# A Trainium2 kernel of two attentions and two ternary feed-forwards: the first attention written out in steps and joined to the feed-forward behind it, with its small sums moved between engines

## The chip, the cores and the metric

The kernel runs on one core of a Trainium2 chip. The metric is the device time of one execution in microseconds (us); the time before is the median of three runs. Engines are named as usual: TensorE (PE, with its weight loads as PEld), VectorE (DVE), ScalarE (ACT), GpSimd (POOL), and SyncE (SP), which issues every DMA here.

## What is computed

`x` and `ctx` are (16, 128, 256) in float32. Four residual blocks follow each other; the first two and the last are those that the change touches.

```python
def first_attention(q, k, v):            # 8 heads over the 256 "times", 16 rows of the 128 per head
    qn, kn = l2norm(q over the 16 rows), l2norm(k over the 16 rows)
    return softmax(5.0 * qn^T kn) applied to v

def ffn(x, w1, w2):                      # rms norm, rounding to 127 levels per row, ternary weights
    h = gelu(gelu(bitlinear(x, w1)))
    return bitlinear(h, w2)

x = x + first_attention(layernorm(x), ctx, ctx)
x = x + ffn(layernorm(x), L0_w1, L0_w2)                        # 256 -> 1024 -> 256
x = x + second_attention(layernorm(x), ctx, Wq, Wk, Wv, Wo)    # 16 heads, 4 of keys and values
x = x + gated_ffn(layernorm(x), w1, w2, w3)                    # 256 -> 2 x 704 -> 256
```

## The kernel before, in words

Line numbers are those of the kernel before, as in its profile.

The program has five parts. `prepare` loads, rounds and transposes the weights. `part_a` is the first attention. Then three parts run in one stream of steps: `part_ffn` "b" (the first feed-forward) from step 0, `part_c` (the second attention) from step 16, `part_ffn` "d" (the last feed-forward) from step 82. Each part is five programs, one per engine. Behind `prepare` and behind `part_a` stands a barrier (`end_part`): every engine drains and waits until all five have come.

**First attention.** The unit of work is a pair of heads of one batch, 4 units per batch, 64 in all. Each engine runs `body` over the units with fixed lags (SCORE = 21, VALUES = 22, COMBINE = 26, ...), counted by semaphores; of the four groups of 16 units, two are written out and two are a loop in hardware (`units`). Per batch:

- SyncE loads x (L292) and ctx (L294), copies the halves of ctx^T to `ctx_t` (L312), stores the split unit rows to a scratch in DRAM (L326), gathers them into stacks of three parts by 16 rows (L303, L306), loads x once more for the residual (L318) and copies the result to `x_rows` (L330), where the feed-forward reads it. 13 issues.
- VectorE: statistics of x (L460, L462, L464), centred and scaled rows (L430), a floor under the length sums (L449), the low half of ctx^T (L437), four copies of values into the stationaries `v_t` (L444, L445), unit rows (L470), their low half (L454), and the combine: four masked products out of the value bank (L412 to L419), a shuffle that brings the sums under the values (L422), and a reciprocal (L425).
- ScalarE: exponentials of 128 x 1024 scores (L361, four per batch), Ln and Exp for the deviation (L370, L372), squares (L378), Ln and Exp of the lengths (L385, L387), the high halves of ctx^T (L394) and of the unit rows (L400).
- TensorE: scores (L487, four matmuls per unit), transposes of ctx into one bank (L498), the length sum over a head's rows (L504, 32-bit, 512 columns), values (L518). A value matmul is 32-bit, has 32 stationary columns and 256 moving ones: 16 columns of values and 16 columns of ones, so that values and softmax sums come out of one matmul. Its output is one of four groups of 32 rows; heads 2r and 2r+1 share the group r and lie in the two halves of the bank. The two heads of a unit lie in two groups:

```python
for k in range(2):
    for j, h in enumerate(heads_of(v)):
        r, half = 32 * (h // 2), D * (h % 2)
        mm = eng.matmul(value_bank(vp)[r:r + 32, half:half + D], v_t[:, vb.lane % 4, k, h, :],
                        probs[:, q, j, k, :], start=(k == 0), stop=(k == 1))
```

- GpSimd: product of the two combined tiles (L346) and the residual add (L349).

**Feed-forwards.** Each step s handles several tiles of 128 rows (one batch each) at different depths: statistics of tile s, rounding of tile s - 2, the wide matmul of tile s - 4, and so on. VectorE runs a chain of one- and two-element instructions per step: in "b" L849 (floor under the variance), in "d" L852 and L855 (the variance times one number plus another), then L866, L876, L885, L891, L903 (the factors of the rounding), and L895 and L896 (a copy of the variance, and minus the mean). Their columns are two: one for a tile at its first rounding, one for a tile five steps older at its second (`pair`). GpSimd takes the power -1/2 (L766) and does the two roundings (L773, L780). ScalarE centres the rows in "d" (L791), VectorE in "b" (L910). In "d", L926 is gate times up (704 columns), L836 the largest absolute value of a row, L872 the residual.

## Time and profile before

| | us |
|---|---|
| median of 3 runs | 829.38 |
| lowest, highest | 828.62, 842.33 |
| profiled execution | 828.9 |
| its span | 827.2 |
| VectorE busy in it | 718.6 (87%) |
| TensorE busy | 681.0 (82%) |
| ScalarE busy | 650.9 (79%) |
| GpSimd busy | 475.1 (57%) |

The span runs from the first to the last instruction; the execution's own time is 1.7 us longer. The shares of busy time are means over stages with different limits, so each stage has to be read by itself. In a row of the timeline, `x8` merges eight instructions of one line, and the number in brackets is the time that the engine was idle ahead of it, with what released it.

### The profile page before, as it was taken

What the parts mean: (1) busy time and instruction counts of PE and PEld (TensorE: products, weight loads), DVE (VectorE), ACT (ScalarE), POOL (GpSimd) and SP (SyncE); (2) the same over time, 40 slices, a digit from 0 to 9 for tenths busy, and PEclk for the clock granted to TensorE, in tenths of its full rate; (3) what the DMA queues carried; (4) which work ended last, traced back from release to release, by engine and by line L of the source; (5) the groups of instructions that cost most, each with busy time, mean ns of one, the idle gap of its engine ahead of it and who ended that gap; (6) DMA issues with size and microseconds to landing.
All of it is one profiled execution on the core that took longest, in us unless ns stands there. A gap on an engine that the chain in (4) does not pass through costs nothing. (4 is left out here: it accounts for less than half of the span.)

```text
span 827.2 us, 16833 instructions
## 1 busy us (share of the span) xinstructions
PE 681.0 (82%) x4627; PEld 412.0 (50%) x4627; DVE 718.6 (87%) x1826; ACT 650.9 (79%) x2170; POOL 475.1 (57%) x639
## 2 busy tenths in 40 slices
PE   0175888888747767999999999999999999977876
PEld 0152333333313335566666666666666666644543
DVE  7667588998569968999999999999999999989996
ACT  0656687877439958999999999999999999977552
POOL 1410022122236778887788788878887888742453
PEclk9997699999969989999999999999999999999997
DMA  8501535544203436779877988788878877864235
GB/s 274 186 1 57 158 115 162 155 150 128 90 23 83 93 78 128 126 132 159 138 140 122 158 142 133 131 152 141 141 129 148 142 141 132 148 117 77 65 98 133
DMA packets 321999, 103.91 MB, mean 126 GB/s; under 512 B 286932, under 2 KB 321142, under 8 KB 321654
## 3 DMA queue, kind: packets, MB, share of 16 engines
q1 hardware_dynamic: 321910, 102.89, 60.4%
q8 instruction: 35, 0.57, 0.3%
q14 instruction: 54, 0.44, 0.2%
HBM read 22.10 MB, written 6.29 MB: 34 GB/s over the span
## 5 line engine op out<-in xcount | busy, mean ns | idle before, releaser
L1328 ACT ACTIVATE psum<-psum,arena 128x256 f32<-128x256 f32 x256 | 136.2, 533 | 18.7 <-DVE arena L1448 18.6
L1404 DVE SCALAR_TENSOR_TENSOR arena<-psum,arena 128x256 f16<-128x256 f32 x256 | 111.0, 475 | 1.1 <-ACT arena L1345 1.1
L1345 ACT ACTIVATE arena<-psum,arena 128x256 f16<-128x256 f32 x256 | 100.6, 476 | 8.4 <-issue 4.2
L1499 PE MATMUL psum<-wq_t,arena 128*128 128x512 f16 x384 | 94.6, 383 | 7.7 <-DMA arena<-arena 4.4
L1537 PE MATMUL psum<-arena 128*128 128x512 f16 x384 | 93.2, 378 | 8.9 <-DVE arena L1431 8.8
L1282 POOL TENSOR_TENSOR arena<-arena 128x512 f32<-128x512 f32 x64 | 81.1, 1267 | 28.0 <-DVE arena L1423 28.0
L1524 PE MATMUL psum<-arena 128*128 128x256 f16 x768 | 94.3, 273 | 1.7 <-DMA arena<-arena 1.0
L1552 PE MATMUL psum<-wo_t,arena 128*128 128x256 f16 x768 | 94.3, 273 | 0.1
L1552 PEld LDWEIGHTS psum<-wo_t,arena 128*128 128x128 f16 x768 | 75.0, 98 | 22.6 <-issue 0.6
L1313 POOL TENSOR_TENSOR arena<-arena 128x512 f16<-128x512 f32 x64 | 74.0, 1157 | 20.0 <-DVE arena L1448 19.9
L1524 PEld LDWEIGHTS psum<-arena 128*128 128x128 f16 x768 | 74.7, 98 | 11.6 <-DMA arena<-arena 2.6
L1423 DVE TENSOR_TENSOR arena<-psum,arena 128x1024 f32<-128x1024 f32 x64 | 78.3, 1224 | 2.4 <-PE psum L1499 2.4
L346 POOL TENSOR_TENSOR arena<-arena 128x256 f32<-128x256 f32 x16 | 11.9, 746 | 115.7 <-DVE arena L425 115.7
L1444 DVE TENSOR_REDUCE arena<-psum 128x4 f32<-128x1024 f32 x64 | 77.9, 1217 | 0.5 <-PE psum L1524 0.4
L361 ACT ACTIVATE arena<-psum 128x1024 f32<-128x1024 f32 x64 | 65.1, 1020 | 16.6 <-PE psum L487 16.6
L1359 ACT ACTIVATE arena<-psum 128x128 f32<-128x128 f32 x256 | 68.5, 305 | 11.8 <-DVE arena L1423 11.8
L518 PE MATMUL psum<-arena 128*32 128x256 f32 x512 | 69.0, 391 | 1.9 <-ACT arena L361 1.7
L1459 DVE SCALAR_TENSOR_TENSOR arena<-psum,arena 128x256 f32<-128x256 f32 x128 | 56.1, 480 | 10.8 <-ACT arena L1394 7.7
L1510 PE MATMUL psum<-wkv_t,ctx_t 128*128 128x256 f16 x384 | 53.7, 276 | 13.3 <-DVE arena L1463 12.4
L1359 ACT ACTIVATION_READ_ACCUMULATOR arena<-psum 128x1 f32 x256 | 61.1, 239 | 0.0
L1316 POOL TENSOR_TENSOR arena<-arena 128x256 f32<-128x256 f32 x64 | 46.4, 724 | 23.4 <-DVE arena L1459 23.4
L1499 PEld LDWEIGHTS psum<-wq_t,arena 128*128 128x128 f16 x384 | 37.4, 98 | 41.3 <-DMA arena<-arena 4.7
(191 smaller groups left out, 1661.2 us busy)
## 6 DMA issues: line engine op xcount, KB each, us to landing
arena<-split_scratch SPq DMA_DIRECT2D x96, 64.0 KB, 2.7
arena<-arena SPq DMA_TRANSPOSE x272, 3.3
arena<-in_x SPq DMA_DIRECT2D x32, 128.0 KB, 2.3
split_scratch<-arena SPq DMA_DIRECT2D x32, 128.0 KB, 1.8
arena<-in_L_ffn_w SPq DMA_DIRECT2D x2, 1024.0 KB, 7.0
x_rows<-in_L_xattn_Wq SPq DMA_DIRECT2D x1, 2048.0 KB, 14.3
ctx_t<-in_L_xattn_Wo SPq DMA_DIRECT2D x1, 2048.0 KB, 12.4
arena<-in_ctx SPq DMA_DIRECT2D x16, 128.0 KB, 2.2
```

The lines of the kernel that those rows point to most:

```text
L1282: eng.tensor_tensor(straight(q_rot[:, :, :]), straight(q_cs[:, 0, :, :]), swapped(q_cs[:, 1, :, :]), ALU.add).then_inc(S["q_rot"], 1)
L1313: eng.tensor_tensor(q_hl(u, 1), flat(q_rot[:, :, :]), q_hl(u, 0), ALU.subtract).then_inc(S["q_lo"], 1)
L1328: last = eng.activation(s_banks(u)[:, h, :], s_banks(u)[:, h, :], ACT.Exp, bias=bias[:, u % 2, h:h + 1], scale=r_q(u)[:, h:h + 1], accum_o ...
L1345: hi = eng.activation(p_hl[:, u % 2, 0, h, :], s_banks(u)[:, h, :], ACT.Copy, scale=share[:, u % 2, h:h + 1])
L1359: last = eng.activation(junk[:, h, :], Q_BANK[:, P * h:P * h + P], ACT.Square, accum_out=sums[:, u % 2, h:h + 1])
L1404: last = eng.scalar_tensor_tensor(p_hl[:, u % 2, 1, h, :], s_banks(u)[:, h, :], share[:, u % 2, h:h + 1], p_hl[:, u % 2, 0, h, :], ALU.mul ...
L1423: eng.tensor_tensor(q_cs[:, :, :, :], Q_BANK.rearrange("p (h d) -> p h d", h=SHARE).unsqueeze(1).broadcast_to([P, 2, SHARE, HEAD_DIM]), tu ...
L1444: eng.tensor_reduce(top[:, u % 2, :], s_banks(u), AX.X, ALU.max).then_inc(S["top"], 1)
L1499: mm = eng.matmul(Q_BANK, y_t[:, b % 2, x, k, :], c.wq_t[:, w, k, SHARE * P * g:SHARE * P * g + SHARE * P], start=(n == 0), stop=(n == 5))
L1524: mm = eng.matmul(s_banks(u)[:, h, :], q_head(u, q, h), k_keys(u, k), start=(n == 0), stop=(n == 2))
L1537: mm = eng.matmul(A_BANK, v[:, u % V_SLOTS, x, k, :], p_t[:, u % 2, w, :, k, :], start=(n == 0), stop=(n == 5))
L1552: mm = eng.matmul(O_BANK, a_t[:, u % 2, a, P * h:P * h + P], c.wo_t[:, w, SHARE * g + h, :], start=(g == 0 and h == 0 and n == 0), stop=(g ...
```

## The change

- `part_a` loses the loop in hardware: all 93 steps are written out, one Python step at a time, and it joins the stream of steps as its first member. The first feed-forward starts at step 93 (`B_START`), the others keep their distance to it. The barrier behind `part_a` goes; the feed-forward waits for each tile of rows (`rows`).
- x is loaded straight into `x_rows`, and GpSimd adds the residual there. The second load of x and the copy to `x_rows` go.
- The stationaries of the values are padded with zeros instead of ones: the even head of a group has its values in columns 0 to 15, the odd head in 16 to 31. Two more stationaries (`ones`) give the sums. Both heads of a group accumulate into the same rows, values in the left half of the bank and sums in the right half, in the same places. Values run once for two units, round all four groups, and `probs` has four slots instead of two.
- The combine is a reciprocal and a multiply on VectorE.
- Squares and both kinds of halves go from ScalarE and VectorE to GpSimd. The halves of ctx are made from ctx itself and are turned by one DMA transpose into `ctx_t`, instead of being made from the transposed ctx.
- The bank of the transposed ctx has two halves in turn, and its values are copied in two instructions instead of four.
- Small moments: the variance is read where the statistics left it (`square_mean`), so that the copy goes; in "b" the mean is subtracted as it is; in "d" GpSimd makes minus the mean, and the two steps ahead of the power.

```diff
-C_START, D_START = 16, 82
+B_START = 93
+C_START, D_START = B_START + 16, B_START + 82
...
-    STATS, RSTD, ROWS, SQUARE, SUM, CTX, CLIP, LENGTH = 3, 4, 5, 5, 8, 10, 9, 11
-    LOAD, CTX_OUT, UNIT, HIGH, LOW, STORE, GATHER = 0, 12, 11, 12, 14, 14, 17
-    SCORE, VALUES = 21, 22
-    RESIDUAL, COMBINE, LAST = 26, 26, 30
-    PEELED = 2
+    LOAD, STATS, RSTD, ROWS, CTX_HALVES, CTX_TURN, SQUARE, SUM, CLIP, CTX, LENGTH = 0, 3, 4, 5, 5, 7, 6, 8, 9, 10, 11
+    UNIT, HALVES, STORE, GATHER, SCORE, VALUES = 11, 12, 14, 17, 21, 23
+    COMBINE, RESIDUAL = 27, 28
+    STEPS = TOTAL + RESIDUAL + 1
...
+        for s in range(STEPS):
+            b = batch(s, CTX_HALVES)
+            if b is not None:
+                p, n = b % 2, b % 4
+                eng.wait_ge(loaded[n], 32 * (b // 4 + 1))
+                wait(eng, ctx_turned[p], 16 * (b // 2))
+                eng.tensor_copy(ctx_hl[:, p, 0, :], yc[:, n, 1, :]).then_inc(S["ctx_high"], 1)
+                eng.wait_ge(S["ctx_high"], b + 1)
+                eng.tensor_tensor(ctx_hl[:, p, 1, :], yc[:, n, 1, :], ctx_hl[:, p, 0, :], ALU.subtract)\
+                   .then_inc(S["ctx_low"], 1)
+            b = batch(s, SQUARE)
+            if b is not None:
+                p, n = b % 2, b % 4
+                eng.wait_ge(S["y"], b + 1)
+                wait(eng, S["lengths"], b - 1)
+                rows = yc[:, n, :, :].rearrange("p a n -> p (a n)")
+                eng.tensor_tensor(sq[:, p, :], rows, rows, ALU.mult).then_inc(S["sq"], 1)
+            b = batch(s, HALVES)
+            if b is not None:
+                p = b % 2
+                eng.wait_ge(S["unit"], b + 1)
+                wait(eng, stored[p], 32 * (b // 2))
+                eng.tensor_copy(halves[:, p, 0, :], unit_rows[:, p, :]).then_inc(S["high"], 1)
+                eng.wait_ge(S["high"], b + 1)
+                eng.tensor_tensor(halves[:, p, 1, :], unit_rows[:, p, :], halves[:, p, 0, :], ALU.subtract)\
+                   .then_inc(S["low"], 1)
+            b = batch(s, RESIDUAL)
+            if b is not None:
+                eng.wait_ge(S["ratio"], b + 1)
+                eng.tensor_tensor(c.x_rows[:, b, :], ratio[:, b % 2, :], c.x_rows[:, b, :], ALU.add)\
+                   .then_inc(S["rows"], 1)
+            yield
...
+                eng.wait_ge(S["values"], 2 * (b + 1))
+                wait(eng, S["ratio"], b - 1)
+                eng.reciprocal(over[:, p, :], value_bank(p)[:, D:2 * D]).then_inc(S["over"], 1)
+                eng.wait_ge(S["over"], b + 1)
+                wait(eng, S["rows"], b - 1)
+                eng.tensor_tensor(ratio[:, p, :], value_bank(p)[:, 0:D], over[:, p, :], ALU.mult).then_inc(S["ratio"], 1)
...
+                for k in range(2):
+                    for what in range(2):
+                        for g in range(4):
+                            q, j = v % PAIRS - 1 + g // 2, g % 2
+                            h = 2 * g + odd
+                            mm = eng.matmul(to[2 * HD * g:2 * HD * (g + 1), D * what:D * what + D],
+                                            ones[:, odd, :] if what else v_t[:, b % 4, k, h, :],
+                                            probs[:, q, j, k, :], start=(odd == 0 and k == 0 and what == 0),
+                                            stop=(odd == 1 and k == 1 and what == 1))
...
-                    eng.tensor_tensor(small["a"][:, slot, cols], small["v"][:, slot, cols], guard[:, 1, cols], ALU.mult)\
-                       .then_inc(S["a"], 1)
-                    eng.wait_ge(S["a"], base["a"] + pairs_before(s, ROWS) + 1 + pairs_before(s, SMALL))
-                    eng.tensor_tensor(small["g"][:, slot, cols], small["a"][:, slot, cols], guard[:, 0, cols], ALU.add)\
-                       .then_inc(S["g"], 1)
...
-                eng.tensor_copy(small["v"][:, t % SLOTS, 0:1], mv[:, t % SLOTS, 1:2]).then_inc(S["mean"], 1)
-                eng.tensor_scalar(minus_mean[:, t % SLOTS, :], mv[:, t % SLOTS, 0:1], -1.0, None, ALU.mult)\
-                   .then_inc(S["mean"], 1)
```

Where instructions move, three places. First, TensorE in the first attention, from the second batch with score, sum and value work side by side. Before (L487 scores, L498 transposes, L504 length sum, L518 values, counted as matmuls):

```order
32 L504 MATMUL psum<-arena,same_head 128x512
33 L518 MATMUL psum<-arena 32x256 x4
34 L487 MATMUL psum<-arena 128x256 x4
35 L518 MATMUL psum<-arena 32x256 x4
36 L487 MATMUL psum<-arena 128x256 x4
37 L518 MATMUL psum<-arena 32x256 x4
38 L487 MATMUL psum<-arena 128x256 x4
39 L518 MATMUL psum<-arena 32x256 x4
40 L487 MATMUL psum<-arena 128x256 x4
41 L498 MATMUL psum<-ident,arena 128x128 x2
```

After (L391 scores, L401 transposes, L405 length sum, L422 values):

```order
34 L405 MATMUL psum<-arena,same_head 128x512
35 L422 MATMUL psum<-arena 32x256 x16
36 L391 MATMUL psum<-arena 128x256 x8
37 L422 MATMUL psum<-arena 32x256 x16
38 L391 MATMUL psum<-arena 128x256 x8
39 L401 MATMUL psum<-ident,arena 128x128 x2
```

Values come in two blocks of 16 per batch instead of four of 4, and scores in two blocks of 8.

Second, GpSimd in the first attention, one batch of the changed kernel (L287, L289 halves of the unit rows, L294 residual, L271, L273 halves of ctx, L281 squares). Before, it held L346 and L349 alone:

```order
55 L287 CAST arena<-arena 128x512
56 L289 TENSOR_TENSOR arena<-arena 128x512
57 L294 TENSOR_TENSOR x_rows<-arena,x_rows 128x256
58 L271 CAST arena<-arena 128x256
59 L273 TENSOR_TENSOR arena<-arena 128x256
60 L281 TENSOR_TENSOR arena<-arena 128x512
```

The squares, which the length sum waits for, stand last in a batch's round.

Third, VectorE in the last feed-forward, one step. Before:

```order
1316 L852 TENSOR_TENSOR arena<-arena 128x2
1317 L855 TENSOR_TENSOR arena<-arena 128x2
1318 L866 TENSOR_TENSOR arena<-arena 128x2
1319 L876 TENSOR_SCALAR arena<-arena 128x2
1320 L882 BN_STATS arena<-x_rows 128x6
1321 L885 RECIPROCAL arena<-arena 128x2
1322 L888 BN_AGGR arena<-arena 128x2
1323 L891 TENSOR_TENSOR arena<-arena 128x2
1324 L895 COPY arena<-arena 128x1
1325 L896 TENSOR_SCALAR arena<-arena 128x1
1326 L901 TENSOR_TENSOR arena<-arena 128x1
1327 L903 TENSOR_TENSOR arena<-arena 128x2
```

After (L778 is the old L866, L784 the residual, L807 and L809 the old L901 and L903):

```order
1255 L778 TENSOR_TENSOR arena<-arena 128x2
1256 L784 SCALAR_TENSOR_TENSOR x_rows<-psum,arena,x_rows 128x256
1257 L788 TENSOR_SCALAR arena<-arena 128x2
1258 L793 BN_STATS arena<-x_rows 128x6
1259 L796 RECIPROCAL arena<-arena 128x2
1260 L799 BN_AGGR arena<-arena 128x2
1261 L802 TENSOR_TENSOR arena<-arena 128x2
1262 L807 TENSOR_TENSOR arena<-arena 128x1
1263 L809 TENSOR_TENSOR arena<-arena 128x2
```

Four small instructions of the step have left VectorE.

## Rows read from the trace of the kernel before

**Rows 1.** Timeline, TensorE, a batch: start, duration (us), line, shape, count [idle before].

```profile
133.48 1.06 PE L518 MATMUL psum<-arena 128*32 128x256 f32 x8
...
140.78 0.44 PE L498 MATMUL psum<-ident,arena 128*128 128x128 f32 x2 [1.12 <-DVE arena L445]
141.05 1.02 PE L504 MATMUL psum<-arena,same_head 128*128 128x512 f32 x2
142.01 1.06 PE L518 MATMUL psum<-arena 128*32 128x256 f32 x8
143.00 0.61 PE L487 MATMUL psum<-arena 48*128 48x256 f16 x4
143.53 1.06 PE L518 MATMUL psum<-arena 128*32 128x256 f32 x8
```

**Rows 2.** Windows: stretch, length, busy PE, PEld, DVE, ACT, POOL, clock, DMA, GB/s.

```profile
251.00:271.00 20.00, 14.89 (x82) 7.15 (x82) 19.83 (x83) 19.62 (x27) 13.48 (x19) 1.00 0.46 94
760.00:800.00 40.00, 33.07 (x221) 19.99 (x219) 39.52 (x161) 21.42 (x42) 18.89 (x29) 1.00 0.32 75
```

**Rows 3.** Timeline, VectorE, one step of the last feed-forward.

```profile
785.77 0.15 DVE L852 TENSOR_TENSOR arena<-arena 128x2 f32<-128x2 f32 x1
...
786.06 0.16 DVE L866 TENSOR_TENSOR arena<-arena 128x2 f32<-128x2 f32 x1
...
787.30 0.15 DVE L895 COPY arena<-arena 128x1 f32<-128x1 f32 x1
...
787.44 0.15 DVE L901 TENSOR_TENSOR arena<-arena 128x1 f32<-128x1 f32 x1
...
789.55 0.15 DVE L852 TENSOR_TENSOR arena<-arena 128x2 f32<-128x2 f32 x1
```

**Rows 4.** Timeline, TensorE, stretches of 0.03 to 0.1 us: rows under way.

```profile
135.01 0.41 PE L518 MATMUL psum<-arena 128*32 128x256 f32 x2
...
135.25 0.39 PE L518 MATMUL psum<-arena 128*32 128x256 f32 x2
...
141.48 0.59 PE L504 MATMUL psum<-arena,same_head 128*128 128x512 f32 x1
```

**Rows 5.** Groups by line and shape, VectorE, 92 to 215 us: busy, mean ns | idle before.

```profile
L425 DVE RECIPROCAL arena<-arena 128x256 f32<-128x256 f32 x14 | 24.5, 1753 | 0.5
...
L419 DVE SCALAR_TENSOR_TENSOR arena<-psum,high_half,arena 128x256 f32<-128x256 f32 x14 | 6.7, 475 | 0.0
```

**Rows 6.** Timeline, VectorE, statistics and unit rows of a batch.

```profile
132.65 0.42 DVE L460 BATCH_NORM_STATS2 arena<-arena 128x6 f32<-128x256 f32 x1
...
133.48 0.69 DVE L470 SCALAR_TENSOR_TENSOR arena<-arena 128x512 f32<-128x512 f32 x1
```

**Rows 7.** Groups by line and shape, GpSimd, whole span.

```profile
L1282 POOL TENSOR_TENSOR arena<-arena 128x512 f32<-128x512 f32 x64 | 81.1, 1267 | 28.0 <-DVE arena L1423 28.0
L1313 POOL TENSOR_TENSOR arena<-arena 128x512 f16<-128x512 f32 x64 | 74.0, 1157 | 20.0 <-DVE arena L1448 19.9
...
L1321 POOL TENSOR_TENSOR arena<-arena 128x256 f16<-128x256 f32 x64 | 43.0, 672 | 5.1
L1286 POOL CAST arena<-arena 128x512 f16<-128x512 f32 x64 | 39.1, 610 | 4.1
...
L1319 POOL CAST arena<-arena 128x256 f16<-128x256 f32 x64 | 25.7, 402 | 4.1
```

**Rows 8.** Source view of L349, GpSimd: shortest, median, longest ns; first and last start.

```profile
L349 POOL TENSOR_TENSOR arena<-arena x16: 722/732/1179, 106.5 to 227.8; 128x256 f32<-128x256 f32 x16
```

**Rows 9.** L412, the first instruction of each combine: source view and timeline.

```profile
L412 DVE TENSOR_SCALAR arena<-psum,high_half x16: 483/484/484, 101.8 to 223.1; 128x256 f32<-128x256 f32 x16
...
196.03 0.48 DVE L412 TENSOR_SCALAR arena<-psum,high_half 128x256 f32<-128x256 f32 x1 [1.83 <-PE psum L518]
```

**Rows 10.** Timeline, around the barrier behind the first attention.

```profile
223.13 0.48 DVE L412 TENSOR_SCALAR arena<-psum,high_half 128x256 f32<-128x256 f32 x1 [1.96 <-PE psum L518]
...
227.82 0.72 POOL L349 TENSOR_TENSOR arena<-arena 128x256 f32<-128x256 f32 x1
...
230.96 0.43 DVE L882 BATCH_NORM_STATS2 arena<-x_rows 128x6 f32<-128x256 f32 x1
```

More of the change, by code:

```diff
@@ L99, in units @@
-def units(eng, total, per, lag, body, before=0, peeled=None):
-    head = peeled or -(-lag // per)
-    for off in range(head * per):
-        body(Unit(0, per, off, total, before))
-    if head < total // per:
-        with eng.Fori(head, total // per) as i:
-            for off in range(per):
-                body(Unit(i, per, off, total, before, head))
-    for off in range(lag):
-        body(Unit(total // per, per, off, total, before))
 class Core:
@@ L261, in part_a @@
     stored = [c.sem(f"a_stored{n}") for n in range(2)]
-    res_loaded = [c.sem(f"a_res{n}") for n in range(2)]
-    ctx_kept = [c.sem(f"a_ctx_kept{n}") for n in range(2)]
-    kept = [c.sem(f"a_kept{n}") for n in range(2)]
+    ctx_turned = [c.sem(f"a_ctx_turned{n}") for n in range(2)]
     S = {n: c.sem("a_" + n) for n in (
-        "var", "rstd", "y", "sq", "lengths", "clipped", "rlen",
-        "unit", "high", "low", "vt", "v_evicted", "ctx_high", "ctx_low",
-        "scores", "exps", "values", "out", "comb", "ratio", "ones")}
+        "var", "rstd", "y", "sq", "lengths", "clipped", "rlen", "unit", "high", "low", "vt", "v_evicted",
+        "ctx_high", "ctx_low", "scores", "exps", "values", "over", "ratio", "rows", "ones")}
@@ L328, in body @@
[L328 to L332 removed]
+            yield
         for p in range(2):
[L334 to L335 removed]
+            eng.wait_ge(ctx_turned[p], 16 * (BATCHES // 2))
@@ L485, in body @@
+        for s in range(STEPS):
+            v = unit(s, SCORE)
+            if v is not None:
+                b, vp = v // PAIRS, v // PAIRS % 2
+                if v % PAIRS == 0:
+                    eng.wait_ge(stacked[vp], 96 * (b // 2 + 1))
+                wait(eng, S["exps"], v - 1)
                 for j, h in enumerate(heads_of(v)):
                     for k in range(2):
-                        mm = eng.matmul(score_banks(q)[:, j, D * k:D * k + D], k_stack[:, vp, h, P * k:P * k + P],
+                        mm = eng.matmul(score_banks(v % 2)[:, j, D * k:D * k + D], k_stack[:, vp, h, P * k:P * k + P],
@@ L506, in body @@
[L506 to L519 removed]
+                eng.wait_ge(S["sq"], b + 1)
@@ L650, in ffn_signals, with part_ffn @@
     return S, turned1, turned2, c.sem("ffn_kept")
-def part_ffn(core, name, up, gate, down, x_dram, attention=None):
+def part_ffn(core, name, up, gate, down, x_dram, rows, attention=None):
     c = core
@@ L879, in vector @@
             if t is not None:
-                if attention is not None:
-                    eng.wait_ge(attention["out"], t + 1)
+                eng.wait_ge(rows, t + 1)
                 eng.bn_stats(stats[:, t % 2, :], c.x_rows[:, t, :]).then_inc(S["stats"], 1)
@@ L1596, in _ @@
         def _(eng):
-            for (sync, _, _, _, _), barrier in parts:
-                sync(eng)
-                barrier(eng)
+            weights[0](eng)
+            barrier(eng)
             in_step(0, eng)
@@ L1604, in _ @@
             constants_pool(eng)
-            for (_, pool, _, _, _), barrier in parts:
-                pool(eng)
-                barrier(eng)
+            weights[1](eng)
+            barrier(eng)
             in_step(1, eng)
@@ L1611, in _ @@
         def _(eng):
-            for (_, _, scalar, _, _), barrier in parts:
-                scalar(eng)
-                barrier(eng)
+            weights[2](eng)
+            barrier(eng)
             in_step(2, eng)
@@ L1619, in _ @@
             eng.wait_ge(core.consts_ready, 1)
-            for (_, _, _, vector, _), barrier in parts:
-                vector(eng)
-                barrier(eng)
+            weights[3](eng)
+            barrier(eng)
             in_step(3, eng)
@@ L1626, in _ @@
         def _(eng):
-            for (_, _, _, _, tensor), barrier in parts:
-                tensor(eng)
-                barrier(eng)
+            weights[4](eng)
+            barrier(eng)
             in_step(4, eng)
```

423 lines of the change are left out of this document (161 added, 262 removed).

## Prediction

> **What bounds the kernel now.** I read the windows by stage first, then the timeline of TensorE, VectorE and GpSimd over one batch of the first attention, then the groups of instructions by line, the source view of two lines, and the end of both small stages. The kernel has five stretches: weights (to about 70 us), first attention (to 227), first feed-forward, second attention (to about 745, untouched by this change), second feed-forward. The change touches the second, the third and the last.
>
> In the steady first attention a batch takes 142.01 - 133.48 = 8.53 us [rows 1]. TensorE carries it: four times 4 score matmuls and 8 rows of value matmuls, then the context transposes and the length sum (140.78 to 142.01, 1.23 us). Ahead of the transposes it stands idle for 1.12 us, until VectorE's L445 has emptied the one bank that they share with ScalarE and VectorE [rows 1]. So the loop is TensorE's work plus one wait on a VectorE that is itself nearly full.
>
> In the first feed-forward ScalarE and VectorE are both full (19.62 and 19.83 of 20 us), in the last one VectorE alone is (39.52 of 40) with a period of 789.55 - 785.77 = 3.78 us [rows 2, 3].
>
> **What a value matmul costs.** This decides the case, since their number doubles: per two units 16 matmuls of 32 stationary columns instead of 8. A 32-bit matmul shows as two rows. The two rows of one length sum, which fills the array, start 0.43 us apart for 512 columns (141.05, 141.48), one behind the other. Of the value matmuls, with 256 columns, two rows start together, at 135.01, and two more at 135.25 [rows 4]. One matmul's own two rows can't be side by side, by the length sum, so each pair is of two different 32-column groups: two groups stream at once, and a round of one row per group costs about 0.22 us. Eight rows in 4 rounds take 143.00 - 142.01 = 0.99 us to the next instruction [rows 1]. The new loop order goes round all four groups, so 32 rows per two units are either 8 rounds (four at once: 0.99 + 4 x 0.216 = 1.85 us) or 16 (two at once: 0.99 + 12 x 0.216 = 3.58 us). Before, two units cost 1.98. The trace never has four groups open at once; I take 1.85, because the two that it shows lose nothing to each other, and keep 3.58 for the range.
>
> TensorEngine Tiling (Array Packing) of the Trainium skill, Performance Considerations, gives 32 stationary columns a fourfold column tiling, which would be 1.85. SBUF — State Buffer of the Trainium skill, Who interferes with whom, gives TensorE a single read port for the moving operand, which speaks against four streams of 32-bit data; by it the price would lie nearer to 3.58. The trace has two streams at no loss and shows nothing of four.
>
> **First attention, new period.** TensorE: scores 0.53 before a value block and 0.44 before more scores (143.53 - 143.00 = 0.53 [rows 1]), so 2 x (0.53 + 0.44) + 2 x 1.85 + 1.23 = 6.9 us. The 1.12 us wait goes, since the bank has two halves and VectorE's part in it falls from five instructions to two.
>
> VectorE loses L412 to L422, L437 and L454 and keeps the reciprocal, 1.75 us, one multiply at L419's 0.48 (0.40 from start to start), and its statistics (132.65 to 133.48, 0.83) and unit rows (0.69) [rows 5, 6]. GpSimd, idle until now but for two instructions per batch, gets six: square 1.27 (as L1282), halves 0.61 + 1.16 (L1286, L1313), context halves 0.40 + 0.67 (L1319, L1321), residual 0.73 (as L349) [rows 7, 8]: 4.84 us. No engine's sum reaches TensorE's 6.9.
>
> But there is a ring through three in-order engines. The last values of a batch release reciprocal and multiply (1.75 + 0.40); behind them in VectorE's queue stand statistics (0.83) and unit rows (0.69), which release GpSimd's halves (1.77); behind these stand residual (0.73), context halves (1.07) and square (1.27), and the length sum of the batch two on waits for that square. With eight handovers of 0.1 that is 8.5 + 0.8 = 9.3 us. From there TensorE needs the sum alone, 142.01 - 141.05 = 0.96, and two value blocks with the scores between, 1.85 + 0.97 + 1.85, to the values that close the ring: 5.6. By the lags of the steps (26 for the values, 32 for the sum, 34 for the values) the ring spans eight steps, two batches: (9.3 + 5.6) / 2 = 7.5 us. GpSimd and VectorE also hinder each other: L349 takes 0.72 at the least and up to 1.18 [rows 8]. I take 7.6 us per batch.
>
> Combining of batch 0 starts at 101.8 and that of batch 11 at 196.03, that of the last at 223.1 [rows 9]. Eleven intervals of 94.2 us become 11 x 7.6 = 83.6: **-10.6**. The last four, without front work, took 27.1 us; by TensorE (2 x (0.97 + 1.85) = 5.6 each, plus 1 us for a late gather) they take 23.6: **-3.5**. The filling of the pipe gets longer: values come one step later and in pairs, and the first low half by GpSimd takes 1.77 us where ScalarE and VectorE took about 1.3: **+1.5**. SyncE issues 11 DMAs per batch instead of 13, one of them a transpose; gather and store keep their lead of several steps, so I cost it at nothing; if the transposes held up the gathers, the wait would show ahead of the scores.
>
> **The barrier.** Before, the last combine starts at 223.13, GpSimd's last add at 227.82, its copy into x_rows lands, and the first statistics of the feed-forward start at 230.96 [rows 9, 10]: 7.8 us. Now VectorE needs 1.75 + 0.40, then stands for the three guards that GpSimd writes behind its last residual (0.73 + about 0.3 with handovers): 3.3 us. **-4.5.** Next in line there is the chain of the first tile, which is unchanged.
>
> **Small moments.** In the first feed-forward two one-element instructions per tile go (L895, L896, 787.44 - 787.30 = 0.14 us where the same lines run in the last stage [rows 3]). ScalarE is as full as VectorE there and keeps its work, so only the filling gains: **-0.4**. In the last one the same two go, and L852 and L855, 786.06 - 785.77 = 0.29 [rows 3]: 0.43 per step, on the engine that has no gap. 21 x 0.29 + 16 x 0.14 = 8.3 us in all; a fifth of the steps lies beside the end of the second attention or in the tail, where other chains end last: **-6.6**. GpSimd takes them, three small ones ahead of its power instruction; it is busy 18.89 of 40 us there [rows 2], ScalarE's centring would wait only if they came over 1 us later than its square ends.
>
> **Sum.** -10.6 - 3.5 + 1.5 - 4.5 - 0.4 - 6.6 = -24.1. The profiled execution took 828.9 us (span 827.2 and 1.7 around it), so 804.8; the median of the runs, 829.4, lies 0.5 higher: 805.
>
> **Rivals.** (a) Two groups at once only. TensorE then needs 6.9 + 2 x 1.73 = 10.4 us per batch and is the bound: 11 x 10.4 - 94.2 = +20.2; the last four 4 x 9.1 - 27.1 = +9.3; filling +3.5; with the other terms (-11.5) that is +21.5, **851 us**, slower. It decides from the moment that a third group has to wait for a stream; break-even is a block of about 2.7 us. For it: no row with more than two. Against it: two lose nothing. (b) GpSimd and VectorE block each other. If each of VectorE's instructions with two SBUF operands or in its fast form, and GpSimd's against it, waits out a good part of the other, as L349 did at 1.18 for 0.72, the ring grows by some 2 us on its four GpSimd members and the multiply, and the period reaches 8.5: the eleven intervals give nothing, **815 us**. Against it: half of GpSimd's work falls beside VectorE's reads of PSUM. SBUF — State Buffer of the Trainium skill, Who interferes with whom, has the pair of ports taken for a whole instruction; L349's slowest instance agrees in kind. (c) The ring is looser than I count, because handovers and starts overlap: TensorE's 6.9 to 7.0 us decides, 11 x 0.65 = 7 us more gain, **797 us**.
>
> **Chances and range.** Forecast 0.52, (a) 0.15, (b) 0.17, (c) 0.14, anything else 0.02. A measurement of this kernel tells about 2% from no change, so faster means under 812.8 and slower over 846. Faster: 0.47 of the forecast's 0.52, all of (c), a third of (b): 0.67. Same: the rest of the forecast, most of (b), a little of (a) in partial form: 0.20. Slower: 0.13. The range must reach (c) with a full gain in the last stage, 794, and (b) with some of (a)'s price, 828; (a) in full stays outside.
>
> **What would show it.** Right: in the first attention four value rows start together, a block of 32 takes about 1.85 us, the period is 7.4 to 7.8 with TensorE idle ahead of the length sum, released by GpSimd; about 3.3 us between the last values and the first statistics of the feed-forward; a step of the last stage at 3.35 us. Wrong: value blocks of 3.5 us and a TensorE without gaps; or GpSimd instructions well above their 0.40 to 1.27 us; or in the last stage VectorE waiting for GpSimd or ScalarE.

## The result, and the profile after

The changed kernel takes **799.43 us** (median of 4 runs, 798.36 to 800.01), against 829.38 shown before and 805 predicted. A fourth run of the kernel before took 838.81, which puts its median at 834.1; its runs scatter from 828.6 to 842.3. The ratio to the kernel before on the same chip is 0.960, 95% interval 0.955 to 0.965: faster. The profiled execution took 800.0 us, its span is 798.3 us, 28.9 shorter than that of before. Line numbers in this part are those of the kernel after, or of the experiment named.

One batch of the first attention on TensorE, in the timeline, answers to [rows 1]:

```profile
126.61 1.12 PE L405 MATMUL psum<-arena,same_head 128*128 128x512 f32 x2 [0.76 <-POOL arena L281]
127.67 1.93 PE L422 MATMUL psum<-arena 128*32 128x256 f32 x32
129.53 1.04 PE L391 MATMUL psum<-arena 48*128 48x256 f16 x8
130.51 1.93 PE L422 MATMUL psum<-arena 128*32 128x256 f32 x32
132.37 1.04 PE L391 MATMUL psum<-arena 48*128 48x256 f16 x8
133.35 0.44 PE L401 MATMUL psum<-ident,arena 128*128 128x128 f32 x2
133.62 1.02 PE L405 MATMUL psum<-arena,same_head 128*128 128x512 f32 x2
```

A block of 32 value rows (L422) lasts 129.53 - 127.67 = 1.86 us to the next instruction. Its rows start in fours, within 0.02 us of each other, eight times 0.22 us apart: four 32-column groups stream at once. The length sum (L405) waits 0.76 us for GpSimd's square (L281), and its next one, at 133.62, not at all. The view of waits, 105 to 175 us, shows both halves of the ring, the chain of work that runs through VectorE, GpSimd and TensorE and comes back to its start two batches later: GpSimd's halves (L287) wait for VectorE's unit rows (L375), and every second length sum waits for the square (engine, line, releaser: us, times, longest):

```profile
POOL arena L287 <- DVE arena L375: 28.3, 10, 5.2
...
PE psum L405 <- POOL arena L281: 3.8, 5, 0.8
```

The period alternates between 6.91 and 7.93 us, mean 7.42, predicted 7.6 (two batches, the ring's span, take 14.84). In the source view the first instruction of each combine is now the reciprocal, 16 times from 103.3 to 206.1 ([rows 9]: 101.8 to 223.1):

```profile
L336 DVE RECIPROCAL arena<-psum x16: 1747/1748/1758, 103.3 to 206.1; 128x256 f32<-128x256 f32 x16
```

The seam between the first attention and the first feed-forward, in the timeline, answers to [rows 10]; 209.24 - 206.08 = 3.16 us instead of 7.83:

```profile
206.08 1.76 DVE L336 RECIPROCAL arena<-psum 128x256 f32<-128x256 f32 x1 [2.35 <-PE psum L422]
207.87 0.42 DVE L339 TENSOR_TENSOR arena<-psum,arena 128x256 f32<-128x256 f32 x1
...
208.38 0.72 POOL L294 TENSOR_TENSOR x_rows<-arena,x_rows 128x256 f32<-128x256 f32 x1 [3.84 <-DVE arena L339]
...
209.24 0.43 DVE L793 BATCH_NORM_STATS2 arena<-x_rows 128x6 f32<-128x256 f32 x1 [0.82 <-POOL arena L660]
```

A step of the last feed-forward on VectorE, which answers to [rows 3], is 763.47 - 760.22 = 3.25 us instead of the 3.78 of the step shown before:

```profile
760.22 0.94 DVE L833 SCALAR_TENSOR_TENSOR arena<-psum,arena 128x704 f32<-128x704 f32 x1
...
762.95 0.13 DVE L802 TENSOR_TENSOR arena<-arena 128x2 f32<-128x2 f32 x1
763.00 0.15 DVE L807 TENSOR_TENSOR arena<-arena 128x1 f32<-128x1 f32 x1
763.07 0.15 DVE L809 TENSOR_TENSOR arena<-arena 128x2 f32<-128x2 f32 x1
763.14 0.41 DVE L755 TENSOR_REDUCE arena<-arena 128x1 f32<-128x256 f32 x1
763.47 0.94 DVE L833 SCALAR_TENSOR_TENSOR arena<-psum,arena 128x704 f32<-128x704 f32 x1
```

Where the 28.9 us of span went, by the starts of the same instructions in both traces:

| stretch | before | after | change | predicted |
|---|---|---|---|---|
| to the first combine | 101.83 | 103.29 | +1.5 | +1.5 |
| eleven intervals | 94.20 | 81.11 | -13.1 | -10.6 |
| last four | 27.10 | 21.68 | -5.4 | -3.5 |
| last combine to first statistics | 7.83 | 3.16 | -4.7 | -4.5 |
| first feed-forward, statistics of tiles 0 to 15 | 44.78 | 42.23 | -2.5 | -0.4 |
| from there to the statistics of the last feed-forward | 453.56 | 453.66 | +0.1 | 0 |
| to the end | 97.88 | 93.15 | -4.7 | -6.6 |

### The profile page after: what moved, and what is told of

Its sections match the earlier page's. It is cut to its first block and busy times, and to the rows that moved or that the text cites. A ratio compares the mean times of both kernels' runs of the same rounds, so it can differ in the third digit from the quotient of the medians.

```text
span 798.3 us, 17290 instructions
## 1 busy us (share of the span) xinstructions
PE 677.3 (85%) x5139; PEld 423.0 (53%) x5139; DVE 661.1 (83%) x1576; ACT 624.3 (78%) x2122; POOL 534.5 (67%) x764
## 3 DMA queue, kind: packets, MB, share of 16 engines
HBM read 20.01 MB, written 6.29 MB: 33 GB/s over the span
## 5 line engine op out<-in xcount | busy, mean ns | idle before, releaser
L305 ACT ACTIVATE arena<-psum 128x1024 f32<-128x1024 f32 x64 | 63.1, 1019 | 33.2 <-PE psum L391 33.2
L1431 PEld LDWEIGHTS psum<-arena 128*128 128x128 f16 x768 | 75.3, 99 | 11.4 <-DMA arena<-arena 1.6
L1266 ACT ACTIVATE arena<-psum 128x128 f32<-128x128 f32 x256 | 68.2, 304 | 10.6 <-DVE arena L1330 10.6
L1223 POOL TENSOR_TENSOR arena<-arena 128x256 f32<-128x256 f32 x64 | 46.3, 724 | 23.7 <-DVE arena L1366 23.6
L422 PE MATMUL psum<-arena 128*32 128x256 f32 x1024 | 61.9, 383 | 0.0
L1444 PEld LDWEIGHTS psum<-arena 128*128 128x128 f16 x384 | 33.7, 97 | 48.0 <-issue 13.6
L1417 PEld LDWEIGHTS psum<-wkv_t,ctx_t 128*128 128x128 f16 x384 | 33.2, 99 | 46.9 <-DVE arena L1370 42.3
## 6 DMA issues: line engine op xcount, KB each, us to landing
x_rows<-in_L_xattn_Wq SPq DMA_DIRECT2D x1, 2048.0 KB, 14.4
```

The costliest lines, as they stand in the source:

```text
L1266: last = eng.activation(junk[:, h, :], Q_BANK[:, P * h:P * h + P], ACT.Square, accum_out=sums[:, u % 2, h:h + 1])
L1417: mm = eng.matmul(KV_BANK[:, KEYS * row:KEYS * row + KEYS], x_t, c.wkv_t[:, w, k, g, :, :].rearrange("p a d -> p (a d)"), start=(n == 0), ...
L1431: mm = eng.matmul(s_banks(u)[:, h, :], q_head(u, q, h), k_keys(u, k), start=(n == 0), stop=(n == 2))
L1444: mm = eng.matmul(A_BANK, v[:, u % V_SLOTS, x, k, :], p_t[:, u % 2, w, :, k, :], start=(n == 0), stop=(n == 5))
```

## Experiments

Times are medians; the ratio is to the kernel before on the same chip. All edits are to the changed kernel.

**1. Two groups, then the other two** (is it the four streams that pay?).

```diff
-for k in range(2):
-    for what in range(2):
-        for g in range(4):
+for two in range(2):
+    for k in range(2):
+        for what in range(2):
+            for g in (2 * two, 2 * two + 1):
```

> The changed kernel with the 16 value matmuls of a block ordered so that two groups of columns are done first and the other two behind them: the same matmuls, but never more than two groups open. Theory (groups stream side by side, each round costs 0.216 us whatever the number of groups): a block takes 16 rounds, about 3.58 us instead of 1.85, TensorE becomes the bound at about 10.4 us per batch, the kernel lands near 845 us (799 + 11 x 3.0 + 4 x 3.46 less what the filling hides). Rival (the order does not matter, a block is limited by something else, such as weight loads or the start of instructions): no change, 799 us.

Measured: 820.16 us, ratio 0.985 (0.979 to 0.990), 20.7 us above the changed kernel. Its block in the timeline:

```profile
129.56 2.82 PE L423 MATMUL psum<-arena 128*32 128x256 f32 x32
132.31 0.94 PE L391 MATMUL psum<-arena 48*128 48x256 f16 x7
```

The block takes 2.75 us, the period 8.68 = 6.91 + 2 x 0.89. So the streams are what is paid for, but not in whole blocks: 2.75 us is 12 rounds of 0.216, not 16. The second pair starts beside the last four rounds of the first: the first row of a group can be told from the others by its length, 0.403 us instead of 0.379, and such rows start twice at 129.56 and twice at 130.46, four rounds later.

**2. One group after the other**, to test that reading.

```diff
-for k in range(2):
-    for what in range(2):
-        for g in range(4):
+for g in range(4):
+    for k in range(2):
+        for what in range(2):
```

> The changed kernel with the value matmuls of two units issued group by group (all eight rows of one 32-column group, then the next) instead of round all four groups. The same 32 rows. Theory (read from the run with two groups first, whose block took 2.75 us, between the 1.85 of eight rounds and the 3.58 of sixteen): a row of a later group may start while rows of an earlier one still stream, as soon as it comes up to the head, and the issue runs some rows ahead; so the block is longer than 2.75 us and shorter than the 32 x 0.216 = 6.9 us of no overlap, about 4.3 us, and the time 845 to 875 us. Rival A: order does not matter beyond pairs, 2.75 us again, 820. Rival B: strictly in order, 6.9 us, period 17, about 950 us.

Measured: 877.86 us (one run).

```profile
128.63 4.59 PE L422 MATMUL psum<-arena 128*32 128x256 f32 x32
133.16 1.04 PE L391 MATMUL psum<-arena 48*128 48x256 f16 x8
```

The block takes 4.53 us. The starts of its rows are at 135.36, .60, .82, 136.03 one by one, from 136.25 on in pairs for twelve rounds, then four more one by one: 20 rounds, where no overlap would take 32. Each group of eight rows begins beside the fifth row of the group before it, which fits experiment 1 (8 + 8 - 4 = 12). The rows don't name their group, but the long first rows of 0.403 us stand where this wants them, at 135.36, 136.26, 137.15 and 138.04; in the changed kernel all four of a block start at 127.67 to 127.69. The period is 12.23 us = 6.91 + 2 x 2.66, and the time lies 3 us above the range of my expectation. Same work and same count of instructions, three orders: 1.86, 2.75, 4.53 us.

**3. Context halves and their transpose two steps later** (take 1.07 us of GpSimd's work out of the ring).

```diff
-... ROWS, CTX_HALVES, CTX_TURN, SQUARE, ... = ... 5, 5, 7, 6, ...
+... ROWS, CTX_HALVES, CTX_TURN, SQUARE, ... = ... 5, 7, 9, 6, ...
```

> The changed kernel with the halves of ctx made two steps later on GpSimd, behind the square instead of ahead of it (and their DMA transpose two steps later). Ring theory (reciprocal, multiply, statistics, unit rows, halves, residual, context halves, square, length sum, two value blocks, over two batches, sets the alternating period of 6.91 and 7.93 us): the ring loses about 1.1 us per two batches, the waits of TensorE ahead of the length sum go, the period is 6.9 to 7.0 throughout, the kernel gains about 11 x 0.5 = 5.5 us, 794 us. Rival (TensorE is the bound on the average and the wait is made up elsewhere): 799 us.

Measured: 795.61 us, ratio 0.955 (0.951 to 0.959). The period is 6.91 eleven times over and no length sum waits for GpSimd; the first combine comes 2.1 us later (105.4), the last 3.0 us earlier (203.09). The ring was the bound, and TensorE's 6.91 stands right behind it. Of the 3.8 us below the changed kernel, 3.0 are the attention's; the two profiles differ by another 1.5 us at the start of the second attention, which this edit doesn't touch (see the last section).

**4. The residual two steps later as well.** RESIDUAL 28 to 30.

> As the run before, and the residual add on GpSimd two steps later too, behind the square. Ring theory: the ring loses another 0.8 us, but TensorE's own 6.9 us is then the bound: the same as the run before within 1 us, 794 us. If the ring were still what sets the period there, it would gain 4 us more.

Measured: 795.89 us, ratio 0.955 (0.951 to 0.959), period 6.91. Nothing more is to be had from the ring.

**5. One step later only.** CTX_HALVES 6, CTX_TURN 8.

> As the run at 795.6 us (context halves and their transpose two steps later), but only one step later. Theory: one step is enough to take the ring off the bound, 6.91 us per batch, and the pipe fills up to 1 us earlier: 794.5 to 796. Rival: the halves then still stand ahead of the square in GpSimd's queue, the ring stays the bound, 799.

Measured: 797.9 us, ratio 0.961 (0.955 to 0.967), with periods of 6.91 and 7.93 as in the changed kernel. The rival holds: the halves still stand ahead of the square in GpSimd's queue, and the last combine starts at 205.93, where the changed kernel has 206.08. That the time is 1.5 us lower has to do with the second attention, by the profiles (last section).

**6. GpSimd's square twice** (add 1.04 us to the ring).

```diff
+eng.tensor_tensor(extra[:, :], rows, rows, ALU.mult).then_inc(S["extra"], 1)
 eng.tensor_tensor(sq[:, p, :], rows, rows, ALU.mult).then_inc(S["sq"], 1)
```

> The changed kernel with the square on GpSimd done twice, the first time into a tile that nobody reads: 1.04 us more GpSimd work per batch. GpSimd has 2 to 3 us of idle time per batch. Ring theory: the ring gets 1.1 us longer per two batches, the period rises by 0.55 us, the kernel by 11 x 0.55 = 6 us, to 805. Rival (only TensorE's load counts, GpSimd's gaps swallow it): 799 us.

Measured: 814.5 us, ratio 0.978 (0.973 to 0.983): 15.1 us for 16 x 1.04. The ring alone would ask for half of that, since it spans two batches. The timeline of TensorE shows what else is in it:

```profile
133.40 2.07 PE L408 MATMUL psum<-arena,same_head 128*128 128x512 f32 x2 [1.75 <-POOL arena L284]
135.40 2.38 PE L425 MATMUL psum<-arena 128*32 128x256 f32 x32
137.71 1.04 PE L394 MATMUL psum<-arena 48*128 48x256 f16 x8
```

After 1.75 us of idleness the length sum takes 2.07 us instead of 1.12 behind the changed kernel's wait, and the value block 2.38 instead of 1.93. The windows of the same stretch have the granted clock at 0.58 (busy PE, PEld, DVE, ACT, POOL, then the clock), where 0.5 is 1.2 GHz:

```profile
128.00:133.00 5.00, 3.65 (x47) 1.96 (x44) 3.00 (x6) 4.03 (x6) 4.84 (x7) 0.99 0.27 78
133.00:137.00 4.00, 3.60 (x26) 1.36 (x30) 2.39 (x7) 1.29 (x4) 2.80 (x4) 0.58 0.54 140
137.00:141.00 4.00, 4.00 (x61) 2.21 (x53) 0.26 (x2) 1.94 (x2) 3.16 (x5) 1.00 0.51 139
```

There are five such gaps of 1.75 us. Behind four of them the clock falls; behind the third, in 146 to 151 us, it doesn't:

```profile
146.00:151.00 5.00, 3.25 (x42) 1.82 (x32) 3.25 (x8) 4.07 (x6) 4.48 (x6) 1.00 0.30 82
151.00:156.00 5.00, 5.00 (x70) 2.55 (x72) 1.59 (x3) 2.33 (x5) 4.16 (x6) 1.00 0.62 184
```

The period with that gap is 8.92 us, the others are 10.32 to 10.56. So one trace separates the two prices: 6.91 + 8.92 = 15.83 us for two batches is what the ring wants (14.84 + 1.04 = 15.88), and the clock adds about 1.6 us each time that it falls.

**7. The same, with TensorE kept at work in the gap.** The two context transposes are done three times over.

```diff
-for k in range(2):
+for k in (0, 1, 0, 1, 0, 1):
     t = eng.transpose(vt_half(b)[:, P * k:P * k + P], ...)
```

> As the run with GpSimd's square done twice (814.5 us), and TensorE's two context transposes of each batch are done three times over (same result), right ahead of the place where it stands idle for the square. Theory: in that run TensorE stood idle for 1.75 us, the granted clock of the 4 us around it was 0.58, and length sum and value block took 2.07 and 2.38 instead of about 0.85 and 1.93 us; with TensorE at work in the gap the clock stays up, and two batches take what the ring wants, 14.84 + 1.04 = 15.9 us, or TensorE's own 13.82 + 2 x 0.88 = 15.6: about 7.95 a batch and 807 to 809 us, less than with the square alone though more work is done. Rival: the clock costs nothing on this path, the ring itself is longer than I count: 814.5 or more.

Measured: 806.93 us, ratio 0.967 (0.960 to 0.975): 7.6 us less than experiment 6, with more work done.

```profile
128.98 0.87 PE L404 MATMUL psum<-ident,arena 128*128 128x128 f32 x6
130.73 1.13 PE L408 MATMUL psum<-arena,same_head 128*128 128x512 f32 x2 [0.88 <-POOL arena L284]
131.79 1.93 PE L425 MATMUL psum<-arena 128*32 128x256 f32 x32
```

```profile
127.00:131.00 4.00, 3.12 (x35) 1.97 (x28) 2.77 (x5) 3.07 (x5) 3.60 (x5) 1.00 0.39 102
131.00:138.00 7.00, 7.00 (x87) 3.79 (x87) 3.38 (x9) 3.86 (x6) 5.61 (x7) 1.00 0.53 150
```

The idle time is 0.88 us, the clock stays at 1.00, the length sum is back at 1.13. Two batches take 7.35 + 8.49 = 15.84 us, the ring's sum again, and the last combine comes 6.9 us earlier than in experiment 6, of the 14.4 us by which that was late. So about half of experiment 6's price was the clock. In the changed kernel itself the wait of 0.76 leaves the clock at 1.00. TensorE: Matmul & The Clock Gate of the Trainium skill (HAM oscillation) says that a stall of TensorE brings the slow clock to the work behind it; four of the five gaps of experiment 6 agree in kind, one doesn't.

**8. Square twice, context halves off the ring.** The edits of 3 and 6 together.

> GpSimd's square done twice, as in the run that took 814.5 us, but with the context halves two steps later (GpSimd) and their transpose with them (SyncE), as in the run that took 795.6. Theory: the square cost 15 us there because it sat in a ring that was the bound and let TensorE's clock fall; off that bound GpSimd has room (about 4.9 + 1.04 of 6.91 us per batch), so the time stays at 795.6 to 798 us, period 6.91. Rival: GpSimd as such is the bound, and each microsecond on it costs whatever the order: 811.

Measured: 801.35 us, ratio 0.965 (0.959 to 0.971), periods of 6.91 and 7.84: between theory and rival, and my expectation was careless. The second square stays in the ring; the edit swaps 1.07 us (context halves) for 1.04. The rule of the ring gives 14.84 - 1.07 + 1.04 = 14.81 us for two batches, and 14.75 was measured. What makes the time 1.9 us longer than the changed kernel's is the filling of the pipe: the first combine starts at 107.22 instead of 103.29.

**9. The barrier put back.**

```diff
 for step in range(D_START + BATCHES + 16):
+    if step == B_START:
+        second(eng)
```

> The changed kernel with the barrier of all engines put back between the first attention and the first feed-forward; nothing else differs. Theory (from the two traces): the 4.7 us that went between the last combine and the first statistics were the shorter combine behind the last values (two VectorE instructions instead of seven) and the copy into the rows that no longer exists; the barrier itself is one handover, and it moves GpSimd's guard writes behind it. So 0.5 to 1.2 us more than the changed kernel: about 800.3 us, first statistics 3.6 to 4.4 us behind the last combine. Rival: the barrier was the price, as my term for it was named: 4.5 us more, 804 us, first statistics 7.5 us behind.

Measured: 798.89 us, ratio 0.958 (0.950 to 0.966), the changed kernel's time. Its seam:

```profile
205.67 1.76 DVE L336 RECIPROCAL arena<-psum 128x256 f32<-128x256 f32 x1 [2.35 <-PE psum L422]
...
209.07 0.43 DVE L793 BATCH_NORM_STATS2 arena<-x_rows 128x6 f32<-128x256 f32 x1
```

209.07 - 205.67 = 3.40 us: at the seam the barrier costs 0.24. It also moves ScalarE's table load (L730) from 212.51 to 217.72, onto the path of tile 5, so the first feed-forward takes 43.58 instead of 42.23 us. The run's time doesn't show that; what covers it stands under the unexpected, below.

**10 and 11. The old small moments**, in the last feed-forward alone, then in both.

```diff
-ffn_d = part_ffn(core, "d", ...)
+ffn_d = part_ffn_before(core, "d", ...)
```

> The changed kernel with the small moments of the last feed-forward as they were before (VectorE's own scale and add of the mean square, its copy of the mean and its negation); the first feed-forward keeps the change. Theory: the step of the last stage goes back from 3.25 to 3.78 us, and the stage's part of the gain as the traces show it, 4.7 to 5.4 us, comes back: about 804.5 us. Rival (the predicted term): 6.6 us more, 806. Second rival: the gain of that stage came from its earlier start only: no more than 1 us.

> The changed kernel with the small moments of both feed-forwards as before. Theory: the first feed-forward gives back 2.5 us more than the run with only the last one undone (its filling step goes from 1.83 to 2.23 us, its rounding pass ahead of the centring one): about 807 us. Rival (the predicted term): only 0.4 us more than that run, 805. If both feed-forward parts are as large as the traces say, this kernel has the gain of the attention and the seam alone: 834.1 less 27, not less 35.

Measured: 804.79 us (ratio 0.964, 0.956 to 0.972) and 806.53 us (0.968, 0.960 to 0.975). The last feed-forward's part is worth 5.4 us, the first one's 1.7. The runs of the two overlap (803.55 to 806.61, and 805.29 to 809.07), so the 1.7 rests on the traces: the statistics of tiles 0 to 15 take 43.98 us with both undone, 42.23 in the changed kernel. With both undone the kernel is still at 0.968 of before, 27 us under the 833.5 of the kernel before on that chip. By the two profiled executions it is less, 828.9 - 805.3 = 23.6 us, and 21.8 of them lie ahead of the first statistics, in the attention and the seam.

**12. Two copies put back** into the last feed-forward's VectorE, of constants that nobody reads.

```diff
+if t is not None and gate is not None:
+    eng.tensor_copy(filler[:, ...], worth[:, 0:1])
+    eng.tensor_copy(filler[:, ...], worth[:, 1:2])
```

> The changed kernel with two one-element copies on VectorE per tile of the last feed-forward, of constants into a scratch that nothing reads, at the place where the copy of the mean square and the negated mean stood before; the rest of the small moments stays on GpSimd. Theory: two things are paid for. The two copies themselves are 0.14 us per step, and they push the two-element product behind them (L809, 0.15 us in every instance, GpSimd's rounding starting just behind it) into GpSimd's rounding, where its fellow took 0.37 us in most steps before: so 0.14 + 0.22 = 0.36 per step, step 3.61 instead of 3.25 us, L809 near 0.37, about 4.5 to 5.5 us in all, 804 to 805. Rival: each instruction costs what its row shows, whatever GpSimd does: step 3.39, 801.6 at most. Second rival: the step isn't VectorE's, 799.4.

Measured: 799.83 us, ratio 0.961 (0.953 to 0.969). The step is 3.37 us, 0.12 longer, and the two-element product is not hit:

```profile
759.40 0.13 DVE L803 TENSOR_TENSOR arena<-arena 128x2 f32<-128x2 f32 x1
759.45 0.15 DVE L806 COPY arena<-arena 128x1 f32<-128x1 f32 x1
759.51 0.14 DVE L807 COPY arena<-arena 128x1 f32<-128x1 f32 x1
...
759.64 0.15 DVE L813 TENSOR_TENSOR arena<-arena 128x2 f32<-128x2 f32 x1
```

The first rival was right. The time alone couldn't tell it from no change (runs of 799.04 to 803.99, the changed kernel at 799.43); the step does. These copies wait for nothing and start 0.06 us earlier than the old ones did, so the product comes 0.24 us behind L803; in experiment 10 it comes 0.34 behind the same product and takes 0.38. The dose missed the point that it was to test.

## Why the prediction held, point by point

**The value matmuls.** The step that decided the case, 8 rounds and 1.85 us per block, came out at 1.86, and the rival with two streams at 3.58 was wrong for the changed kernel. The choice of 1.85 had no row with four streams behind it, so this was a bet that came true. Experiments 1 and 2 show that this is a matter of order, and that even its own order of two at a time wouldn't have cost 3.58 but 2.75 us, near the rival's own break-even of 2.7, with a time still 1.5% under that of before. TensorEngine Tiling (Array Packing) of the Trainium skill, Performance Considerations, agrees with the 1.86. The single port for the moving operand in SBUF — State Buffer of the Trainium skill, Who interferes with whom, costs nothing here with four 32-bit streams.

**The period.** Ring (7.5, taken as 7.6) and TensorE's sum (6.9) were both right in place: 7.42 and 6.91. Two batches were to take 9.3 + 5.6 = 14.9 us by the ring and take 14.84, but luck has a part in that. The members outside TensorE and their eight handovers come to 8.5 us instead of 9.3, and 0.6 stand in the ring that the prediction left out: two VectorE copies of context values (L355, L356, 132.56 to 132.97), which by the kernel's text wait for the same value block as the reciprocal and stand ahead of it. What remains over-sized is the 0.1 us that I had added for hindrance between GpSimd and VectorE. The square takes a mean of 1067 ns and not L1282's 1267. In the groups by line (busy us, mean ns) the new instructions lie at or near the taken values:

```profile
L289 POOL TENSOR_TENSOR arena<-arena 128x512 f16<-128x512 f32 x16 | 18.6, 1163 | 1.3
L281 POOL TENSOR_TENSOR arena<-arena 128x512 f32<-128x512 f32 x16 | 17.1, 1067 | 0.7 <-DVE arena L344 0.7
...
L294 POOL TENSOR_TENSOR x_rows<-arena,x_rows 128x256 f32<-128x256 f32 x16 | 11.7, 731 | 16.2 <-DVE arena L339 16.2
L287 POOL CAST arena<-arena 128x512 f16<-128x512 f32 x16 | 11.7, 731 | 42.4 <-DVE arena L375 42.4
```

Only L287 is longer (731 for 610). Rival (b), the blocked ports, is not what this stage shows. Rival (c), TensorE as the bound, is what experiments 3 and 4 make of it. Where the term of -10.6 was off it was by 11 x 0.18 = 2.0 us of period and 0.5 us in where the alternation begins and ends.

**The last four.** -5.4 for -3.5: I had added 1 us for a late gather that didn't come, and the last interval is 4.57, shorter than the others at 5.7.

**The seam.** -4.67 for -4.5, but under the wrong name. The term was headed by the barrier; experiment 9 shows that the barrier itself is 0.24 us. By the two traces the rest is a combine of two VectorE instructions instead of seven, and a copy into `x_rows` that no longer exists. No run undid these two apart.

**The first feed-forward.** The step that failed most: "ScalarE is as full as VectorE there and keeps its work, so only the filling gains", -0.4. The stage gave 2.5 us, and undoing it in experiment 11 costs 1.7. While the pipe fills (tiles 2 to 4) the step is 1.83 us instead of 2.22, and 2.22 again in experiment 11; and in the last five tiles it is 3.27 instead of 3.33 to 3.52. Its centring pass, 16 times, was 514 ns and is 346 in the median, before and after:

```profile
L910 DVE TENSOR_SCALAR arena<-x_rows,arena x16: 344/514/517, 232.7 to 279.7; 128x256 f32<-128x256 f32 x16
```

```profile
L817 DVE TENSOR_SCALAR arena<-x_rows,arena x16: 321/346/350, 210.5 to 255.2; 128x256 f32<-128x256 f32 x16
```

In experiment 11 it is 515 ns again. Why it is longer there was not tested. And 0.8 of the 2.5 us stay open: with the old small moments back, the stretch takes 43.98 us and not the 44.78 of before.

**The last feed-forward.** The stage gave 4.7 us (5.4 by experiment 10) instead of 6.6, and both factors of the term were off. The step that I had read before, 3.78 us, is a short one: from L926 to L926, six steps in a row from 776.30 on take 4.03, 3.78, 3.79, 4.03, 4.03 and 4.03 us, and the changed kernel's 3.25 each. So a steady step gave 0.53 or 0.78 us, not 0.43. Against that, gate times up (L833) now waits for ScalarE (L742), 3.6 us in five instances from 712 to 798, where its like L926 never waited; ScalarE waits for TensorE (L863), and that for a DMA. The last step even grew from 2.99 to 4.44 us. "A fifth of the steps" was too little for what lies beside other work.

By the profiled execution (800.0 for 804.8) the whole was 4.8 us too cautious: attention 4.4, seam 0.2 and first feed-forward 2.1 more than predicted, the last one 1.9 less. Two misses of opposite sign, 2.1 too little and 1.9 too much, cancel in that. The time lies within the range of 794 to 828.

## To carry to other kernels

Matmuls of 32 stationary columns are cheap only in turn: issue them round all four column groups, row by row, since the same 32 rows took 1.86, 2.75 or 4.53 us by order alone. When several in-order engines hand a batch round, add up the ring and divide by the batches that it spans; a change of lags that takes one link out (here 1.07 us by two steps) can be worth as much as a faster instruction, and the version of experiment 3, at 795.6 us, is the fastest measured here, though its interval overlaps that of the changed kernel. A wait of TensorE costs more than its length where the clock falls behind it. And a step read from a trace should be read over several neighbours: the one of 3.78 us had neighbours of 4.03.

## What the runs showed that I had not expected

**The clock behind a wait.** 1.75 us of idleness in the middle of full work brought 1.2 GHz for the rows behind it in four cases of five, 0.76 or 0.88 us never did, and filling the gap with useless transposes won 7.6 us.

**A hidden 1.5 us at the start of the second attention.** There TensorE stands idle and comes back at 1.2 GHz, but for different times. Windows of the changed kernel, then of experiment 9:

```profile
282.00:290.00 8.00, 6.91 (x35) 4.50 (x34) 4.69 (x12) 2.88 (x19) 7.60 (x11) 0.57 0.45 92
```

```profile
282.00:286.00 4.00, 3.67 (x16) 1.68 (x15) 2.76 (x9) 1.11 (x7) 3.86 (x6) 0.57 0.52 99
286.00:292.00 6.00, 4.61 (x36) 3.10 (x35) 4.66 (x10) 4.41 (x23) 5.66 (x8) 1.00 0.54 109
```

The third interval between units there is 7.80 to 7.82 us in the profiles of the changed kernel and of experiments 6 and 10, and 6.29 to 6.32 in the ten others and before. In those three profiles the stretch at 1.2 GHz around the third interval is about twice as long as in the others, some of which have none there. That is how the profiled execution of experiment 9 could lose 1.3 us in the first feed-forward and show none of it, and why differences of 1.5 us between single profiles of this kernel aren't to be explained by the edit.

**Two engines on one path for tiny instructions.** In the kernel before, the two-element product L903 took 0.16 us, and where it came late against GpSimd's rounding 0.37. In the source view (shortest, median, longest ns) of the kernel before, of the changed kernel's same product, and of experiment 10:

```profile
L903 DVE TENSOR_TENSOR arena<-arena x42: 146/165/374, 234.7 to 818.4; 128x2 f32<-128x2 f32 x22, 128x1 f32<-128x1 f32 x20
```

```profile
L809 DVE TENSOR_TENSOR arena<-arena x42: 146/153/156, 212.3 to 789.2; 128x2 f32<-128x2 f32 x22, 128x1 f32<-128x1 f32 x20
```

```profile
L1142 DVE TENSOR_TENSOR arena<-arena x21: 151/373/377, 720.3 to 795.9; 128x2 f32<-128x2 f32 x11, 128x1 f32<-128x1 f32 x10
```

Two instances of before, the first long and the second short, with GpSimd's rounding beside them:

```profile
779.60 0.48 POOL L773 TENSOR_SCALAR arena<-arena 128x256 f16<-128x256 f32 x1 [0.53 <-DVE arena L891]
779.71 0.37 DVE L903 TENSOR_TENSOR arena<-arena 128x2 f32<-128x2 f32 x1
...
787.41 0.53 POOL L773 TENSOR_SCALAR arena<-arena 128x256 f16<-128x256 f32 x1 [0.53 <-DVE arena L891]
787.50 0.16 DVE L903 TENSOR_TENSOR arena<-arena 128x2 f32<-128x2 f32 x1
```

All long instances, 11 before and 12 in experiment 10, start 0.11 us behind GpSimd's pass and end with it to within 0.01 us. The short ones beside a pass, 3 and 2, start 0.09 behind it, and there the pass takes 0.53 instead of 0.48. In experiment 10 a step is 4.03 us, 0.78 above the changed kernel's, though its four small instructions count for 0.43. It is the effect that my rival (b) feared in the attention, working the other way in the feed-forwards. Experiment 12 was to prove the mechanism and missed its timing: its products start 0.00 to 0.01 us behind the pass and take 0.15. So that the product waits for GpSimd's rounding is read from the rows, not shown by an edit. SBUF — State Buffer of the Trainium skill, Who interferes with whom, has an exclusive lock between a VectorE instruction with two SBUF operands and a GpSimd instruction that reads SBUF; the long instances agree with it in kind. The short ones also start behind the pass and don't wait for its end, so the lock as stated there is not all that these rows show.
